# Last layer of a four-layer kernel: other places within an image for its tail, its split, the shifted queries and the router's exponential

## The reference, cut to what matters

```python
t = t + _L3_attn_ref(_ln_t(t), ...)      # per image: 1024 tokens, 32 channels, 4 heads of 8
    qkv = (x @ W_qkv + b_qkv)
    att = softmax(q k^T / sqrt(32)); out = att v; out @ W_proj + b_proj
t = t + _L3_ffn_ref(_ln_t(t), ...)       # router of 8 experts, the best 2, weights rescaled to sum 1
    router_probs = softmax(x @ router_w + router_b)
    top_p, top_i = top_k(router_probs, 2); top_p = top_p / sum(top_p)
    expert_out = einsum('bnd,edc->bnec', x, expert_w) + expert_b
    sum over the two of top_p * expert_out
```

## Time and profile before

| what | value |
|---|---|
| median of 3 runs | 8382.55 us (8376.12 to 8406.81) |
| profiled execution | 8411.8 us, its span 8410.0 us |
| last layer | from about 4400 us to the end |
| busy share of the span, PE, DVE, ACT, POOL | 78%, 63%, 62%, 26% |
| mean granted TensorE clock | 0.861 |

### The profile page before, as it was taken

The page is one execution under the profiler, slowest core; times in us unless marked ns, Lnnn a source line. Parts: engine busy times, 40 slices in busy tenths (PEclk is TensorE's granted clock), DMA queues, the critical chain, the costliest instruction groups (busy, mean ns, idle before and its releaser), DMA issues. The chain is left out here.

```text
span 8410.0 us, 159293 instructions
## 1 busy us (share of the span) xinstructions
PE 6565.4 (78%) x48272; PEld 2699.4 (32%) x48272; DVE 5284.7 (63%) x9974; ACT 5206.3 (62%) x8588; POOL 2201.0 (26%) x3329
## 2 busy tenths in 40 slices
PE   3467888888888888755647888888888888888887
PEld 3223444444444444333432222222222222222222
DVE  5544555555555555433328788777878778787785
ACT  0116778788778778600005777777777777777776
POOL 0022222222222222111112333333333333333333
PEclk7668898999999899856658999999999999999998
DMA  1010000000000000011110000000000000000000
GB/s 70 11 40 9 6 6 6 5 6 6 5 6 6 5 6 6 8 23 26 20 14 7 7 9 7 9 7 8 8 7 9 7 9 7 7 9 7 9 7 5
DMA packets 502064, 92.31 MB, mean 11 GB/s; under 512 B 475742, under 2 KB 501295, under 8 KB 501423
## 3 DMA queue, kind: packets, MB, share of 16 engines
q1 hardware_dynamic: 500399, 86.02, 5.6%
q10 hardware_dynamic: 1152, 0.05, 0.0%
HBM read 52.47 MB, written 33.56 MB: 10 GB/s over the span
## 5 line engine op out<-in xcount | busy, mean ns | idle before, releaser
L2036 DVE TENSOR_REDUCE d_peaks<-d_p_k 128x1 f32<-128x512 f32 x4096 | 2616.8, 685 | 523.7 <-PE d_p_k L1880 486.5
L1747 ACT ACTIVATE d_wt<-d_p_s 128x512 f32<-128x512 f32 x4096 | 2197.3, 608 | 679.8 <-PE d_p_s L1851 670.2
L735 ACT ACTIVATE b_sq<-b_p_s 128x1024 f32<-128x1024 f32 (+3 forms) x1536 | 1273.8, 829 | 374.8 <-PE b_p_s L831 368.6
L744 ACT ACTIVATE b_wt<-b_sq 128x1024 f32<-128x1024 f32 (+3 forms) x1536 | 1331.2, 867 | 225.1 <-POOL b_sq L703 225.1
L1864 PE MATMUL d_p_o<-d_wt,d_v_pad 128*32 128x512 f32 x8192 | 1200.9, 661 | 4.2 <-ACT d_o_sb L1752 3.5
L1880 PE MATMUL d_p_k<-d_kT,d_qT 64*128 64x512 bf16 x4096 | 853.7, 411 | 416.7 <-DVE d_peaks L2036 394.3
L831 PE MATMUL b_p_s<-b_qT,b_kT 128*128 128x512 bf16 (+3 forms) x3072 | 794.9, 366 | 203.8 <-ACT b_sq L735 200.0
L703 POOL TENSOR_SCALAR_AFFINE_SELECT b_sq<-b_sq 128x256 f32<-128x256 f32 x1024 | 424.3, 420 | 1925.9 <-ACT b_sq L735 1925.9
L1851 PE MATMUL d_p_s<-d_qT,d_kT 64*128 64x512 bf16 x4096 | 841.5, 407 | 66.0 <-ACT d_wt L1747 32.9
L843 PE MATMUL b_p_o<-b_wt,b_v_pad 128*32 128x512 f32 (+3 forms) x6144 | 706.3, 536 | 1.2 <-ACT b_wt L744 1.2
L1851 PEld LDWEIGHTS d_p_s<-d_qT,d_kT 64*128 64x128 bf16 x4096 | 200.7, 94 | 1260.2 <-ACT d_wt L1747 854.2
(11 more groups left out here) (278 smaller groups left out, 9285.2 us busy)
## 6 DMA issues: line engine op xcount, KB each, us to landing
w<-in_L_conv_W SPq DMA_DIRECT2D x64, 128.0 KB, 2.1
t<-rows SPq DMA_DIRECT2D x64, 128.0 KB, 1.8
b_x_in<-t SPq DMA_DIRECT2D x64, 128.0 KB, 2.6
t<-b_result SPq DMA_DIRECT2D x64, 128.0 KB, 2.2
c_x_in<-t SPq DMA_DIRECT2D x64, 128.0 KB, 2.8
t<-c_result SPq DMA_DIRECT2D x64, 128.0 KB, 2.7
d_x_in<-t SPq DMA_DIRECT2D x64, 128.0 KB, 2.8
d_x_keep<-t SPq DMA_DIRECT2D x64, 128.0 KB, 2.9
```

Source lines behind the costliest of these rows:

```text
L735: act.activation(sq[:, n % SQ_RING, :, 0:m], p_s[n % 2][:, :, 0:m], ACT.Square).then_inc(squared, 1)
L744: act.activation(wt[:, n % RING, :, 0:m], sq[:, n % SQ_RING, :, 0:m], ACT.Silu, scale=1.0 / D).then_inc(weighed, 1)
L1747: act.activation(wt[:, n % RING, :], tile(n)[:, :], ACT.Exp, scale=SCALE).then_inc(s_used, 1)
L2036: dve.tensor_reduce(peaks[:, m, r:r + 1], bank((m, r))[:, :], X, ALU.max).then_inc(k_used, 1)
```

## The change

The same instructions run, at other places of a window. In PE's and ACT's misc tables `attT` goes from group 4 to 3, `qkv0` and `qkv1` from 6 and 7 to 4 and 5, `high` from 5 to 6, `xl4T` from 9 to 7, `route` from 10 to 8, the experts from 11 and 12 to 9 and 10, `low` from 9 to 11, the key and query transposes from 13, 14, 15 to 12 to 15, one in each; `proj` goes from 5 to 4 and `o0` from 10 to 11. ACT's `exp_router` goes from group 12 to 9. DVE's small operations follow. On POOL, `split_second` now stands ahead of the low half's `shift_parts`.

```diff
-S_MISC = {3: ("xlT",), 4: ("attT",), 5: ("high",), 6: ("qkv0",), 7: ("qkv1",), 9: ("low", "xl4T"), 10: ("route",),
-          11: ("experts0", "experts1"), 12: ("experts2", "experts3"), 13: ("k0",), 14: ("k1",), 15: ("q0", "q1")}
-K_MISC = {2: ("o1",), 5: ("proj",), 10: ("o0",)}
+S_MISC = {3: ("xlT", "attT"), 4: ("qkv0",), 5: ("qkv1",), 6: ("high",), 7: ("xl4T",), 8: ("route",),
+          9: ("experts0", "experts1"), 10: ("experts2", "experts3"), 11: ("low",), 12: ("k0",), 13: ("k1",), 14: ("q0",),
+          15: ("q1",)}
+K_MISC = {2: ("o1",), 4: ("proj",), 11: ("o0",)}
...
                 if "prep" in win.on:
                     split_first(win)
+                    split_second(win)
                 if "next" in win.on:
                     shift_parts(win.image("next"), win.slot("next"), 0)
-                if "prep" in win.on:
-                    split_second(win)
...
-                    if "prev" in win.on and a == 12:
+                    if "prev" in win.on and a == 9:
                         exp_router()
...
-                        if m == 10:
+                        if m == 8:
                             residual()
+                        if m == 9:
+                            centre(p, x4, total2, centred2, ln2_step, xl4_made)
                         if m == 11:
-                            centre(p, x4, total2, centred2, ln2_step, xl4_made)
-                        if m == 13:
                             sum_squares(p, square2, squares2, ln2_step, ln2_square)
+                        if m == 17:
+                            less_most()
+                        if m == 20:
+                            probabilities()
                         if m == 21:
-                            less_most()
-                        if m == 24:
-                            probabilities()
-                        if m == 25:
                             compared(4)
-                        if m == 26:
+                        if m == 22:
                             compared(2)
                             step(compared(1))
-                        if m == 27:
+                        if m == 23:
                             ranked()
-                        if m == 28:
+                        if m == 24:
                             mixed()
-                        if m == 29:
+                        if m == 25:
                             scaled()
...
-                        if m == 20:
+                        if m == 22:
                             attended(o, 0)
...
-                        if m == 16:
+                        if m == 12:
                             split_high()
-                        if m == 19:
+                        if m == 14:
                             split_middle()
-                        if m == 22:
+                        if m == 18:
                             split_low()
```

## The result

The changed kernel takes 7835.6 us (median of four runs, 7809 to 7841) where the one before takes 8379.3 (median of four, 8374 to 8407): ratio 0.934, 95% interval 0.931 to 0.937. It is 544 us faster, 6.6%. Forecast were 7955 us and at best 7860.

What follows compares the result with a forecast made beforehand. Waits, not a full engine, were taken to bound the kernel. Group terms summed to 54.2 us a window for 61.2, 427 us over 61 windows: 7985 profiled, 7955 on the median's scale, range 7860 to 8035 (0.63).

Steps and rivals of the forecast that it cites:

- Three waits: PE waits of 1.72, 2.60 and 2.18 us in groups 1, 9 and 13, each followed by a clock fall.
- The exponential: Router's exponential moved to ACT's group 9: DVE's wait for it, 3.1 us an image, goes.
- "low": Group 9: PE's wait of 2.60 us for POOL's shift goes with "low" in group 11 and `split_second` earlier.
- the place of `combine`: Started behind m = 25, it ends over 1 us before DVE's centring, which then takes 0.43 instead of 1.78.
- POOL's order: `split_second` ahead of the low shift, named with the later place of "low" as removing the 2.60 us wait.
- the term for groups 9 to 12: Experts 3.9 twice, group 11 4.2 to 4.8, group 12 3.4 to 3.7; taken as 16.2 us, before 18.1.
- The other rows of the table: Forecast 9.9 us for groups 0 to 2, 18.8 for 3 to 8, 9.3 for 13 to 15.
- The rule that DVE hides all its small work: Low rule: a group takes 2.79 or its fullest engine's need; 51.9 a window, 7815 us, cut at 7860.
- The stalls move: Rival, 0.17: PE idles in group 11 and the clock falls again; gain 4.0 us a window, 8139 us.
- Casts beside POOL: Rival, 0.08: split casts slow fourfold, like the centring, costing 2.0 us; gain 5.0 a window, 8078 us.
- A late `xl4`: Rival, 0.07: 1 us of lateness and one clock fall, 2.5 us; gain 4.5 a window, 8108 us.
- POOL's queue: Rival, 0.05: `split_first` late behind `normalise` stops DVE at `split_middle`, then PE; not faster, 8474 us at 7 us lateness.

Runs made afterwards that it cites:

- e1: The kernel before with only the router's exponential on ACT moved one group earlier, behind group 11 instead of 12: 8216.2 us, ratio 0.978.
- e2: The kernel before with only "low" turned one group later, in group 10 beside the route instead of group 9: 8156.8 us, ratio 0.972.
- e3: The kernel before with both the exponential one group earlier and "low" one group later: 7999.3 us, ratio 0.953.
- e6: The changed kernel with `mixed` and `scaled` back at m = 28 and 29, so `combine` starts four pairs later: 7990.2 us, ratio 0.953.
- e4: The changed kernel with POOL's old order, `split_second` behind the low shift, "low" still in group 11: 7819.9 us, ratio 0.933.
- e8: The changed kernel with a second, unread `ranked` reduction (0.61 us) on DVE at m = 28, in group 14: 7823.0 us, ratio 0.933.
- e7: The changed kernel with a second, unread `ranked` reduction (0.61 us) on DVE at m = 23, in group 11: 7870.8 us, ratio 0.938.
- f1: The changed kernel with the sum of the tail's squares at m = 10 instead of 11: 7845.8 us, ratio 0.934.
- f2: f1 with `o0` and `attended` of the first half moved to group 14 (m = 28): 7848.9 us, ratio 0.934.
- e5: The changed kernel with the exponential behind group 10 instead of 9, probabilities still at m = 20: 8013.6 us, ratio 0.955.

## Where the forecast was right, and where its size was off

**Three waits, each with a fall of the clock behind it.** This was the claim, and the runs bear it out one by one. The exponential is worth 182 us (e1), "low" 238 (e2), together 22 less than their sum (e3), the place of `combine` 157 (e6). These three make 577 where the whole change gains 550 in the layer, 5% more. The clock has its share in each: of the 550 us PE's idle time gives 331 and the clock 219. A window's share of the clock is 1.6 us in e1 and 1.5 in e2, where the prediction had put 1.4 and 1.7 for a fall.

**POOL's order.** The forecast named it beside the later place as what frees "low". It gives no gain (e4).

**The step that failed** is the term for groups 9 to 12: 15.4 to 16.4, taken as 16.2, measured 14.72. Of the 1.5 us, 1.2 are in groups 11 and 12 (about 8.4 in the sum, 7.18 measured). The forecast added each group up by itself, and took group 11 and 12 as a plain one of 2.79 plus almost all their small DVE work. (Its four terms make 16.3 at the most, not 16.4.) DVE's timeline, from group 10 to the end of group 12, shows three things against that:

```profile
7697.96 1.29 DVE L2036 TENSOR_REDUCE d_peaks<-d_p_k 128x1 f32<-128x512 f32 x2 [0.27 <-PE d_p_k L1880]
7699.17 0.21 DVE L2107 TENSOR_REDUCE d_col<-d_expo 128x8 f32<-128x64 f32 x1
...
7700.39 1.29 DVE L2036 TENSOR_REDUCE d_peaks<-d_p_k 128x1 f32<-128x512 f32 x2 [0.51 <-PE d_p_k L1880]
...
7701.99 1.28 DVE L2036 TENSOR_REDUCE d_peaks<-d_p_k 128x1 f32<-128x512 f32 x2
7703.19 0.21 DVE L2124 TENSOR_TENSOR d_above<-d_prob 128x64 f32<-128x64 f32 x1
7703.33 0.24 DVE L2125 TENSOR_TENSOR d_above<-d_prob 128x64 f32<-128x64 f32 x1
7703.46 0.20 DVE L2124 TENSOR_TENSOR d_above<-d_prob 128x32 f32<-128x32 f32 x1
7703.56 0.20 DVE L2125 TENSOR_TENSOR d_above<-d_prob 128x32 f32<-128x32 f32 x1
7703.89 0.26 DVE L2058 RECIPROCAL d_share<-d_p_k 128x16 f32<-128x16 f32 x1
7704.18 0.29 DVE L2061 TENSOR_TENSOR d_att<-d_p_k,d_share 128x128 f32<-128x128 f32 x1
7704.39 1.28 DVE L2036 TENSOR_REDUCE d_peaks<-d_p_k 128x1 f32<-128x512 f32 x2
7705.59 0.61 DVE L2128 TENSOR_REDUCE d_rank<-d_above 128x64 f32<-128x448 f32 x1
7706.31 1.29 DVE L2036 TENSOR_REDUCE d_peaks<-d_p_k 128x1 f32<-128x512 f32 x2
...
7709.69 2.52 DVE L2036 TENSOR_REDUCE d_peaks<-d_p_k 128x1 f32<-128x512 f32 x4
```

- A plain group is not full on DVE. Its four peak tiles take 2.44 us to the start of what follows (7668.41 to 7670.85 in the timeline above), out of 2.79. So 0.35 us of small work hides in each group. e8 shows it: a reduction of 0.61 recorded (0.52 start to start), in a group without any, costs nothing. Six peak tiles follow it without a gap (3.76 us) before DVE idles again, so the next group's slack takes the rest.
- Recorded durations of neighbours overlap. L2124 and L2125 at 7703.19 to 7703.56 are recorded at 0.20 to 0.24 and start 0.10 to 0.14 apart; the pair of peaks is recorded at 1.29 and takes 1.20. A sum of recorded means is too large.
- A queue carries work over a group's border. DVE's own share of group 11 lasts 4.32 us (7701.99 to 7706.31), inside the 4.2 to 4.8 of the forecast, but PE begins group 12 after 3.45. DVE's first pair of a group starts 0.71 us behind PE's start of group 11, 1.58 behind that of group 12, 1.23 of 13 and 0.64 of 14: it falls behind in group 11 and catches up in 12 and 13. For groups 9 to 12 together DVE takes from 7694.48 to 7709.69, 15.21 us with 1.02 in waits for PE, against PE's 14.72.

The other rows of the table are too long by 0.2, 0.2 and 0.4 us. For the last the forecast went by ACT, not DVE: four exponentials and a copy of 1.02, 3.0 to 3.2 us a group. Groups 14 and 15 last 2.78 each, and ACT shows the second of the three things, recorded times that overlap. From copy to copy it takes 2.82 us, where the records add up to 3.11:

```profile
7713.21 1.03 ACT L1743 ACTIVATE d_qT<-d_p_s 128x1024 bf16<-128x1024 bf16 x1
7714.12 2.08 ACT L1747 ACTIVATE d_wt<-d_p_s 128x512 f32<-128x512 f32 x4
7716.03 1.09 ACT L1743 ACTIVATE d_qT<-d_p_s 128x1024 bf16<-128x1024 bf16 x1
```

Group 13 lasts 3.36, and that is where DVE catches up. What makes the first two rows 0.2 too long was not looked into. 2.33 us too much a window, by 61 windows, are 142 of the 144 us between forecast and measurement on the scale of the profiled executions (7985 and 7841); the partial windows at the end gave 20 more, and the mean window gave about as much less than the one that I measured.

**The range.** The rule that DVE hides all its small work gave 51.9 us a window and 7815 us, and the window now lasts 51.87. That match is luck in part: the rule's terms are 9.3, 18.2, 15.4 and 9.0, measured are 9.66, 18.57, 14.72 and 8.92, two above and two below. Still, a range down to 7815 would have held the time. I had it and cut it off at 7860, on the ground that the old groups 3 to 8 "deny" it, since they keep 1.3 of their 2.25 us. That argument was not sound: those groups also hold the projections and the transposes on PE and their copies on ACT, so what they last beyond six plain groups need not be DVE's work. e7 shows what a full group does charge, 0.35 of 0.61.

**The rivals.** *The stalls move:* no. The longest wait of PE ahead of an L1880 in the window is 0.55 us, and the clock stays 1.00. The Trainium skill (TensorE: Matmul & The Clock Gate, section A second HAM failure mode) would have let frequent short idling swing the clock; this window, with nine waits of 0.3 to 0.55 us on PE and a clock of 1.00, disagrees. *Casts beside POOL:* L2085 slows from 420 to 581 ns, 0.16 us a window and not 2.0, and f1 shows that even this cost nothing. The factor of four was the wrong measure: the centring's length follows the end of POOL's instruction beside it (last section), and the copies beside the cast are short. *A late `xl4`:* 0.41 us of wait for PE (forecast at worst 0.3), since group 6 lasts 2.78 and not 3.1; the chain itself takes 3.22 of the 3.23 forecast. It was worth nothing by f1. *POOL's queue:* `left` came 0.03 us ahead of DVE's asking, where the working had 0.2; it held by less than forecast.

## What to carry to other kernels

- In a loop that several engines share and in which none is full, look for single waits of PE; here they were 1.7 to 2.6 us long. Each cost itself and, in most windows, a piece of slow clock behind it, and each can be tested alone by moving one operation, in either direction; here three of them added up to the gain within 5%. Where the same matmuls run in both kernels, PE's busy time tells the clock's share.
- Before small work is charged, measure the slack of a plain stretch from start to start, not from recorded durations, and let neighbours share it: charge only what a whole run of groups has too much. Where a bound rests on "the check denies it", see that the check has the same engine at its limit.
- Room that is free for an operation on SBUF alone need not be free for one that reads a PSUM bank which PE fills (e8 and f2; the reason was not tested).

## What the runs showed of the hardware

- **Two SBUF inputs beside GpSimd.** L2049 takes 0.42 us alone and 1.78 and 2.07 beside `combine`. The Trainium skill (GPSIMD Engine Reference, section Specifications) says that such DVE instructions contend with GpSimd; the runs agree (mean 1461 ns before and 1497 in e3, 425 after and in e5). A cast with one input, L2085, suffers as well: 0.59 for 0.42, the copies on POOL 0.60 for 0.40. The peaks, which read PSUM, stay at 1.28 to 1.29 beside POOL.
- **The slowed instruction ends 0.28 us behind POOL's.** Before, POOL's first L1703 ends at 8220.66 and L2049 at 8220.95; in e6 at 7807.29 and 7807.57; after, L1671 at 7690.17 and the cast L2085 at 7690.45. In the layer 57 of the 64 L2049 before and 62 of the 64 L2085 after start beside such an instruction, and the median is 0.28 us each time. So the length follows what POOL has left to do, and not a factor. It is not so beside every instruction: the cast L2081 runs beside POOL's L1659 (128x8, 1.64 us) in 61 windows after the change and keeps its 0.42.
- **The granted clock** falls behind a single wait of PE of 1.7 to 2.6 us in a stretch where PE is busy otherwise (1.72, 2.60 and 2.18 before, 2.17 in e5, 2.01 in e6), to between 0.50 and 0.62 of full speed over 3 us. In the next slice it is at 0.88 to 1.00 before and 1.00 in e5, but still 0.50 in e6. It does not fall every time. From 4450 to 7700, the three microseconds that begin 1 us behind the wait are below 0.8 in 33 of 53 cases in e3 (waits near 1.7 us), in 41 of 58 in e5 (near 2.2) and in 47 of 49 in e6 (near 2.0). The length of the wait alone does not decide it. Nine waits of 0.3 to 0.55 us in the window shown, four of them within 7 us, leave it at 1.00. By run the mean clock from 4500 to 7600 goes with the waits left: 0.92 before, 0.95 (e1, e2), 0.97 (e3, e5), 0.96 (e6), 0.99 after.
